# GpSimd instead of VectorE makes the low halves of the odd query and key tiles in the projection

## What is computed

```
xn  = layernorm(x)                                  # x: 2 sequences x 2048 tokens x 256
q, k, v = split(xn @ Wqkv)                          # 16 heads of 16
q, k = rope(q), rope(k)                             # rotary embedding
attn = softmax(causal(q @ k.T * scale)) @ v
moe  = sum over the top 2 of 10 gates of gate * (xn @ expert_w[e] + expert_b[e])
out  = x + attn @ Wout + bout + moe
```

## Time and profile before

| | |
|---|---|
| median of three runs | 1004.11 us |
| span of the profiled execution | 1022.0 us |
| projection, steps 1 to 6, one step | 11.40 us |
| last instruction of the projection on DVE | ends at 133.5 us |
| busy over the whole span: PE, DVE, ACT, POOL | 89%, 83%, 71%, 45% |
| busy from 50 to 75 us: PE, DVE, ACT, POOL | 20.6, 24.3, 14.9, 19.5 of 25 us |

### The profile page before, as it was taken

One profiled execution on the slowest core, in us unless ns is written; L12 is line 12 of the kernel. 1 busy time (PEld: TensorE's weight loads), 2 busy tenths in 40 slices (PEclk: granted clock), 3 DMA queues, 4 the chain that ended last, 5 costly groups with the idle time before them and its releaser, 6 DMA issues. The chain is left out here.

```text
span 1022.0 us, 22104 instructions
## 1 busy us (share of the span) xinstructions
PE 907.5 (89%) x7874; PEld 392.7 (38%) x7874; DVE 847.0 (83%) x1096; ACT 728.5 (71%) x1542; POOL 462.9 (45%) x588
## 2 busy tenths in 40 slices
PE   2888446999999999999999899999999999999888
PEld 1554311332432334344434444344434333322257
DVE  6999789899899878886889688877888799894846
ACT  3556200788788878787888788778878788789822
POOL 4677568565201253344833474354132245355610
PEclk8999755999999999999999999999999999999979
DMA  9766810301200324244413542255334321112113
GB/s 324 267 248 248 276 46 11 105 3 38 68 2 2 115 78 121 76 133 147 125 53 98 151 143 74 72 162 132 77 85 125 90 62 49 32 58 64 37 52 124
DMA packets 82084, 106.65 MB, mean 104 GB/s; under 512 B 10000, under 2 KB 59064, under 8 KB 80952
## 3 DMA queue, kind: packets, MB, share of 16 engines
q1 hardware_dynamic: 74488, 85.83, 26.1%
q0 software_dynamic: 6528, 17.83, 6.8%
q10 hardware_dynamic: 960, 1.57, 0.5%
HBM read 67.37 MB, written 37.50 MB: 103 GB/s over the span
## 5 line engine op out<-in xcount | busy, mean ns | idle before, releaser
L1275 DVE TENSOR_REDUCE blk<-psP 128x2 f32<-128x1024 f32 (+2 forms) x576 | 641.4, 1162 | 103.5 <-PE psP L1421 53.7
L1221 ACT ACTIVATE probs<-psS 128x512 f32<-128x512 f32 (+3 forms) x1280 | 589.2, 541 | 162.2 <-PE psS L1458 153.1
L1458 PE MATMUL psS<-Qs,Ks 50*128 50x512 f16 (+3 forms) x1280 | 332.0, 353 | 24.5 <-ACT probs L1221 15.4
L1418 PE MATMUL psP<-Ks,Qs 48*128 48x512 f16 (+3 forms) x1280 | 299.6, 363 | 31.7 <-DVE blk L1275 20.5
L1514 PE MATMUL psO<-probs,Vs 128*32 128x512 f32 (+3 forms) x2560 | 300.3, 547 | 6.0 <-POOL probs L1124 4.9
L1124 POOL TENSOR_SCALAR_AFFINE_SELECT probs<-probs 128x512 f32<-128x512 f32 x128 | 88.1, 689 | 356.3 <-ACT probs L1221 317.4
L1458 PEld LDWEIGHTS psS<-Qs,Ks 50*128 50x128 f16 x1280 | 96.4, 93 | 256.6 <-ACT probs L1221 149.2
L1418 PEld LDWEIGHTS psP<-Ks,Qs 48*128 48x128 f16 x1280 | 80.4, 94 | 132.9 <-DVE blk L1275 94.8
L1421 PE MATMUL psP<-later,eye 64*128 64x128 bf16 x1024 | 103.6, 223 | 0.0
L1514 PEld LDWEIGHTS psO<-probs,Vs 128*32 128x32 f32 x2560 | 52.9, 108 | 86.4 <-issue 65.2
L1421 PEld LDWEIGHTS psP<-later,eye 64*128 64x128 bf16 x1024 | 78.1, 98 | 19.6 <-issue 1.7
(11 more groups left out here) (170 smaller groups left out, 729.3 us busy)
## 6 DMA issues: line engine op xcount, KB each, us to landing
xn<-we_scratch SPq DMA_DIRECT2D x72, 256.0 KB
expert_scratch<-xn SPq DMA_DIRECT2D x36, 256.0 KB
v_scratch<-vst SPq DMA_DIRECT2D x8, 1024.0 KB, 4.0
qk_scratch<-part SPq DMA_DIRECT2D x32, 256.0 KB, 4.0
Vs<-v_scratch SPq DMA_DIRECT2D x16, 512.0 KB, 3.9
Qs<-qk_scratch SPq DMA_DIRECT2D x168, 32.0 KB
Ks<-qk_scratch SPq DMA_DIRECT2D x168, 32.0 KB
acc<-x SPq DMA_DIRECT2D x8, 512.0 KB, 9.2
```

The costliest lines, as they stand in the source:

```text
L1221: nc.scalar.activation(probs[u % NPR][:, h, q0:CH], psS[:, k % SB, q0:CH], ACT.Exp, scale=exp_scale).then_inc(s_read[k % SB], 1)
L1275: nc.vector.tensor_reduce(out, src, AX.X, ALU.max).then_inc(item_ok[slot], 1)
L1418: ins = pe.matmul(psP[:, slot, at:at + w], Qs[r][rows, qt // CT, p, t * P:(t + 1) * P], Ks[r][rows, kc, p, 0:w], start=True, stop=True)
L1458: pe.matmul(psS[:, k % SB, q0:CH], Ks[r][rows, kt // CT, p, kt % CT * P:(kt % CT + 1) * P], Qs[r][rows, c, p, q0:CH], start=True, stop=Tru ...
```

## The change

`low(s, k0 + 1)` is put behind `low(s, k0)` on GpSimd, and DVE's `split` with its three calls goes away:

```diff
                         nc.gpsimd.tensor_tensor(rot[k0 + 1], rot[k0 + 1], turn[k0][:, 1, :], ALU.add
                                                 ).then_inc(sum_ok[k0 + 1], 1)
                         low(s, k0)
+                        low(s, k0 + 1)
...
-            def split(s, k):
-                dve.wait_ge(high_ok[k], ONE + s + 1)
-                nc.vector.tensor_tensor(part[k][:, 1, :], rot[k], part[k][:, 0, :], ALU.subtract
-                                        ).then_inc(split_ok[k], 1)
...
                     rope(s, j, 1)
-                    if not first:
-                        split(s - 1, 3)
...
                         norm_c(s + 2, b)
-                    split(s, 1)
...
             nc.vector.tensor_tensor(lg[:, :, :], lg[:, :, :], wide(gm[:, :]), ALU.subtract).then_inc(gate_in, 1)
-            split(LAST, 3)
```

## The result

| | before | after |
|---|---|---|
| median | 1004.2 us (998.8 to 1004.8, 4 runs) | 1012.05 us (1010.7 to 1012.9, 4 runs) |
| ratio to before | | 1.0079, 95% interval 1.0052 to 1.0106 |
| deviation to deviation | 11.40 us | 12.32 us (one of five 13.43) |
| `sent`, the gates' last operation, starts at | 121.69 us | 129.45 us |
| first reduction of the attention stage (`blk<-psP`, DVE) starts at | 137.44 us | 145.41 us |

The change makes the kernel 7.9 us slower, which is within 1%. The forecast was 1011.0. A second group of ten runs of the same changed kernel, beside 23 of before, gave 1.0072 (1.0046 to 1.0098).

A forecast was written before the change was run, and what follows sets the result against it. DVE bounded the step at 11.40 us; after the change a loop of waits across engines would, at 12.34. Five steps gave +4.7 us, the projection's end +2.2: +6.9 on the 1004.11 median, so 1011.0 us, range 1006 to 1016.

The forecast's parts named there:

- The loop: Projection step: waits among ACT, GpSimd and DVE from deviation to deviation make it 12.34 us instead of 11.40; chance 0.66.
- The choice between 0.03 and 0.25 us: Rope 2 behind GpSimd's low 3: DVE's time to see the signal, bounded by these values; 0.25 taken.
- the rival in which low_e wins: Projection step: low_e is asked for before GpSimd's second sum; deviations 11.2 us apart, 1005.3 us in all; chance 0.15.
- The end of the projection: After the last deviation: rope 2 of step 7 2.1 us later, holds +0.1, together +2.2 us.
- The stores cost nothing: SP's stores in a step: tile 1 earlier, tile 3 about 0.9 us later, at no cost.
- the rival of the clock: Projection: PE's granted clock falls to half, +32 us over five steps, 1043 us in all; chance 0.04.
- up to 18.8 us a step: PE's work of a projection step at half the clock, 6.5 us over the 12.34, in five steps.
- The busy share that spoke against it: PE's work filling 76% of the 12.34 us step, far nearer to 82% than to 45%; argued against a clock fall.
- handed on whole: Routing and attention stage: the attention stage starts behind the routing, so it takes over the whole delay, +2.2 us.
- 4.7 and 2.2: In us: five projection steps at +0.94 each, and the delay after the last deviation; together +6.9.
- The base of the sum: Whole kernel: the difference found on the profiled execution of 1022.0 us is carried over to the median, 1004.11 us.
- The price of the hold: DVE's low_e beside GpSimd's sum: a two-input operation of this size ends 0.55 us after the GpSimd operation.

The follow-up runs named there:

- tile 1: The changed kernel with only tile 1's low part on GpSimd and DVE's split of tile 3 back: 11.74 us a step, 1.0036 of before.
- tile 3: The changed kernel with only tile 3's low part on GpSimd and DVE's split of tile 1 back: 11.99 us a step, 1.0043 of before.
- short-loop kernel: The changed kernel with high 1 ahead of the deviation, high_e behind high_x, low_e at step's end, weight store one step later: 9.84 us a step, 0.9927 of before.
- kernel with one input: The changed kernel with low_e reading one SBUF tensor instead of two, writing a scaled copy of the weights: 12.06 us a step, 1.0055 of before.

## Why the prediction was right

**The loop.** Its terms held one by one. From the deviation at 45.28, in us:

| event | predicted | measured |
|---|---|---|
| low 1 | 0.89 to 2.05 | 0.89 to 2.04 |
| `less` ends | 2.07 | 2.06 |
| normal_x starts | 2.11 | 2.10 |
| high 2 starts | 4.69 | 4.69 |
| low 3 ends | 7.65 | 7.64 |
| rope 2 starts | 7.90 | 7.89 |
| low_e asked for, ends | 9.03, 10.65 | 9.03, 10.65 |
| next deviation | 12.34 | 12.33 |

Only rows of before went into it, since every length in the loop was one of a like instruction there: the earlier trace rows priced `less`, and split 1's end 0.55 after the sum priced low_e. The tile 1 and tile 3 kernels confirm that these are the two delays, and the short-loop kernel that nothing else kept the step above GpSimd's own 9.84 us.

**The choice between 0.03 and 0.25 us** for DVE to see GpSimd's signal decided between the forecast and the rival in which low_e wins. It measured 0.25 (low 3 ends at 52.92, rope 2 starts at 53.17). Taking the row of the same instruction, though behind another engine, was the better guide than ACT's.

**The end of the projection.** Rope 2 of step 7 comes 17.72 us behind the last deviation (17.85 predicted). The gates' end comes 129.45 - 95.67 = 33.78 behind it, against 121.69 - 90.01 = 31.68: +2.10, as the +2.2 in the sum. The stores cost nothing, as predicted: in neither profile of after does ACT wait for one.

**Two terms that were not in the sum.** One of the five intervals was 13.43 us in the first profile and 12.33 in the second. In the first the granted clock was 0.90 and 0.53 from 68 to 80 us, and PE's 12 matmuls of queries and keys from 75.9 us on took 4.59 us instead of 2.75. Rope 2 of that step, in the first profile and then in the second:

```profile
78.85 1.23 DVE L560 TENSOR_TENSOR turn<-psQ,trig 128x1024 f32<-128x1024 f32 x1 [1.32 <-PE psQ L709]
```

```profile
77.81 1.23 DVE L560 TENSOR_TENSOR turn<-psQ,trig 128x1024 f32<-128x1024 f32 x1 [0.28 <-POOL part L345]
```

It waited for PE where it otherwise waits for low 3, and began 1.04 us later. This is the rival of the clock in small: its sign (a clock below 1.00) came, its price did not, 1.1 us in one execution and none in the other. The step that failed there is "up to 18.8 us a step": it took PE at half the clock for all five steps, and the rows have it so for about 6 us of one. The busy share that spoke against it doesn't tell the stretches apart either: PE was busy 2.88 of 6 us from 56 to 62 us at a clock of 1.00, and 3.18 of 6 from 68 to 74 at 0.90. The second term is the routing behind the gates, which the sum handed on unchanged. It took 141.57 - 129.45 = 12.12 us against 133.29 - 121.69 = 11.60, but 12.73 and 12.48 in the second profiles of before and after, where the clock there was 0.63 and not 0.76. So it differed by up to 1.1 us among four executions of two kernels, whichever kernel ran.

**The sum beside the traces.** From the first profile of before to the first of after the attention stage starts 7.97 us later: 5.66 at the last deviation (1.1 of it the clock's), 2.10 at the gates, 0.52 in the routing, and -0.31 behind it. From second to second it is 5.93: 4.40, 2.09, -0.25 and -0.31. The last part contradicts "handed on whole": from L700 to the first reduction it takes 4.15 us in both profiles of before and 3.84 in both of after, and why stays open. So the terms of the forecast, 4.7 and 2.2, are shown, to 0.1 to 0.3 us; that its sum of 6.9 lies only 1 us from the 7.85 between the medians is partly luck, since clock, routing and the end of the attention stage each move an execution by 1 us or more.

**The base of the sum.** Carrying a difference from a span of 1022.0 to a median of 1004.1 was right, but by luck, for a reason that the prediction did not know: the 18 us were in a stage that the change does not touch. Had they been in the projection, the step of 11.40 would have been wrong as well.

**The price of the hold.** The forecast of 0.55 us was met: low_e ended at 55.93, 0.55 after the sum. The 12.45 us a step that the prediction's reading of the Trainium skill, "SBUF — State Buffer", section "SBUF: two separate sides", gives (0.11 more) was not: the step took 12.32. The 0.66 us in that reading is not low_e's length alone, since low_e was asked for 0.11 us before a sum ended in the earlier trace rows as well; a split that began while GpSimd was idle (109.45 us in the trace of before) took 0.68, so a held one does end sooner behind the hold than its own length. "Two-input operations" as the class that is held was too narrow, as the kernel with one input shows; it did no harm, since the loop's other operations kept their lengths (statistics 1.39 us, 1.40 in the earlier trace rows).

## What to carry to other kernels

Before work is moved from the engine that is full to one that seems to have time, follow one step through the orders of all engines: what the moved work now waits for, and what is queued behind it there. Here the full engine's relief turned into waiting because a high part stood behind a wait on ACT and because GpSimd and DVE hold each other; with four operations moved out of those places, the same change gave 0.7% where it had lost 0.8% (three of the four moves were not tried without the change). And where one execution's span lies 1.8% above the median, find the stage that has it before trusting any of its rows.

## What the runs showed of the hardware

- GpSimd can be kept out while DVE issues two-input SBUF operations back to back: a mask took 7.18 to 7.20 us, until 0.5 us behind the last of them, in four profiles, and 0.85 or 0.86 in eight others. With a pause after every fourth it took 0.79, and the runs of before scattered over 1.4 us instead of 9.
- An operation on 128x4 elements is held like a large one: `less` took 0.68 us beside GpSimd's low part and 0.16 without.
- The one-input SBUF operation of low_e was held as well, and ended 0.29 us behind GpSimd's sum at two different starts; the two-input one 0.55 behind. The statistics, one SBUF input too, were not: 1.39 us beside GpSimd's low part.
- In the changed kernel's first profile PE's granted clock fell to 0.53 (near the lower of its two levels, 1.2 and 2.4 GHz) from 74 to 80 us, after a stretch in which PE was busy 3.18 of 6 us; that cost 1.1 us there. In its second profile it was 0.87 and 0.85 in the stretches from 68 and from 74 us, and nothing was lost.
- From the end of GpSimd's low part to the start of the rope that waits for it DVE took 0.25 us; from DVE's `less` to normal_x on ACT it was 0.04.
